# ScalarE's copy of the turned runs between the scalings of two merge tiles, and VectorE's exponentials' low part after the values' low part

## What is computed

```python
x_cat = concatenate([node_feat[src], node_feat[dst], edge_feat], axis=-1)
r = x_cat @ Wr.T + br
q = (node_feat @ Wq.T + bq).reshape(n, H, D)
k = (r @ Wk.T + bk).reshape(e, H, D)
v = (r @ Wv.T + bv).reshape(e, H, D)
a = einsum('ehd,ehd->eh', q[dst], k) * scaler
amax = segment_max(a, dst)
ae = exp(a - amax[dst])
asum = segment_sum(ae, dst)
out = segment_sum(v * (ae / asum[dst])[..., None], dst).reshape(n, H * D)
```

## Time and profile before

| | us |
|---|---|
| median of 3 runs | 1853.32 |
| lowest and highest run | 1849.9, 1858.21 |
| profiled execution, its own time | 1842.91 |
| its span, first to last instruction | 1841.1 |
| busy in it: PE | 1623.5 (88%) |
| DVE | 1296.4 (70%) |
| ACT | 1026.3 (56%) |
| POOL | 697.5 (38%) |

### The profile page before, as it was taken

How to read it: one execution, slowest core, us unless ns; L and a number is a source line. 1 busy time by engine, 2 the same in 40 slices (tenths; PEclk the granted TensorE clock), 3 DMA queues, 4 the chain that set the end, 5 groups by cost and what they waited for, 6 DMA issues and landing times. The chain is left out here.

```text
span 1841.1 us, 26829 instructions
## 1 busy us (share of the span) xinstructions
PE 1623.5 (88%) x7162; PEld 1189.9 (65%) x7162; DVE 1296.4 (70%) x3259; ACT 1026.3 (56%) x3674; POOL 697.5 (38%) x723
## 2 busy tenths in 40 slices
PE   7989979999999999999999999999993777888523
PEld 6867767777777777777777777777772333444311
DVE  5875728887888878887888788878883455322688
ACT  3882225777677777777777767776773344100011
POOL 0001224555555555555555555555551000000033
PEclk9999989999999999999999999999995888999855
DMA  5664327566666666666666666666653324000001
GB/s 181 205 227 154 124 86 238 194 207 212 208 205 201 216 211 207 199 217 212 210 201 212 213 216 199 213 215 201 214 161 130 128 88 137 0 1 0 23 12 44
DMA packets 129670, 300.28 MB, mean 163 GB/s; under 512 B 29088, under 2 KB 50727, under 8 KB 129522
## 3 DMA queue, kind: packets, MB, share of 16 engines
q0 software_dynamic: 63600, 180.17, 29.1%
q1 hardware_dynamic: 60738, 107.59, 19.4%
q10 hardware_dynamic: 5184, 10.81, 1.6%
HBM read 271.40 MB, written 66.58 MB: 184 GB/s over the span
## 5 line engine op out<-in xcount | busy, mean ns | idle before, releaser
L1196 ACT ACTIVATE wv<-vv,expd 128x64 f32<-128x64 f32 x1256 | 316.6, 334 | 2.8
L1208 ACT ACTIVATE old<-old,expd 128x64 f32<-128x64 f32 x1256 | 307.7, 334 | 0.0
L1140 POOL DMA_INDIRECT merge<-new,put_id x157 | 161.1, 1026 | 273.7 <-DVE new L1366 242.1
L1409 PE MATMUL psK<-M_hi,efT_hi 128*128 128x512 f32 x628 | 253.4, 403 | 6.4 <-ACT efT_hi L1166 6.4
L1409 PE MATMUL psV<-M_hi,efT_hi 128*128 128x512 f32 x628 | 255.9, 408 | 0.0
L1410 PE MATMUL psV<-M_lo,efT_hi 128*128 128x512 f32 x628 | 249.7, 398 | 0.0
L1410 PE MATMUL psK<-M_lo,efT_hi 128*128 128x512 f32 x628 | 249.2, 397 | 0.0
L1111 POOL DMA_INDIRECT old<-merge,dst_id x157 | 156.0, 994 | 138.3 <-DMA merge<-new,put_id 112.6
L1111 POOL DMA_INDIRECT kv<-kv_table,src_id x157 | 157.1, 1001 | 72.7 <-issue 47.8
L1182 ACT ACTIVATE expd<-diff 128x32 f32<-128x32 f32 (+1 forms) x79 | 18.1, 229 | 293.9 <-DVE diff L1347 293.9
L1111 POOL DMA_INDIRECT qc<-q_table,dst_id x157 | 155.6, 991 | 53.0 <-issue 46.9
(11 more groups left out here) (271 smaller groups left out, 3404.6 us busy)
## 6 DMA issues: line engine op xcount, KB each, us to landing
efT<-in_ef_turned_dram SPq DMA_DIRECT2D x78, 512.0 KB, 5.0
merge<-empty ACTq DMA_DIRECT2D x4, 2640.0 KB, 9.7
rows<-merge SPq DMA_DIRECT2D x40, 264.0 KB, 3.7
row_block<-dst_rows POOLq DMA_DIRECT2D x13, 768.0 KB, 5.8
dst_line<-dst_rows SPq DMA_DIRECT2D x78, 128.0 KB, 2.7
end_line<-end_rows SPq DMA_DIRECT2D x78, 128.0 KB, 4.1
kv_table<-kv_out SPq DMA_DIRECT2D x10, 512.0 KB, 3.2
raw<-in_L_gnn_Wr_dram SPq DMA_DIRECT2D x12, 256.0 KB, 5.1
```

Source lines behind the costliest of these rows:

```text
L1140: pool.indirect_dma_start(out=merge[2 * (p % 2) + u][:, :], out_offset=bass.IndirectOffsetOnAxis(ap=put_id[:, t:t + 1], axis=0), in_=new[p ...
L1196: act.activation(wv[:, u, h * DH:(h + 1) * DH], vv[p % 2][:, u, h * DH:(h + 1) * DH], ACT.Copy, scale=expd[p % 2][:, u, 0, h:h + 1]).then_ ...
L1208: act.activation(rows, rows, ACT.Copy, scale=expd[p % 2][:, u, 1, h:h + 1]).then_inc(old_scaled, 1)
L1409: pe.matmul(out[:, :], efT_hi[b][:, u, c, :], Me_hi[:, c, col:col + D], start=c == 0, stop=False)
```

## The change

In ACT's loop scale_old takes one tile instead of a pair. The copy of the runs stands between the scaling of the first and of the second old tile; before, it stood behind both. In DVE's loop the low part of the weighted values of pair p - 2's first tile comes ahead of the low part of its exponentials; before, behind it. Instructions, shapes, buffers and waits of each instruction stay as they are.

```diff
-            def scale_old(p):
-                for u in range(tiles_of(p)):
-                    act.wait_ge(old_in[p % 2], landed(p))
-                    for h in range(H):
-                        rows = old[p % 2][:, u, h * DH:(h + 1) * DH]
-                        act.activation(rows, rows, ACT.Copy, scale=expd[p % 2][:, u, 1, h:h + 1]).then_inc(old_scaled, 1)
+            def scale_old(t):
+                p, u = t // 2, t % 2
+                act.wait_ge(old_in[p % 2], landed(p))
+                for h in range(H):
+                    rows = old[p % 2][:, u, h * DH:(h + 1) * DH]
+                    act.activation(rows, rows, ACT.Copy, scale=expd[p % 2][:, u, 1, h:h + 1]).then_inc(old_scaled, 1)
...
                 if p >= 2:
-                    scale_old(p - 2)
+                    scale_old(2 * p - 4)
                 if 1 <= p <= PAIRS:
                     copy_runs(p - 1)
+                if p >= 2 and tiles_of(p - 2) == 2:
+                    scale_old(2 * p - 3)
+                if 1 <= p <= PAIRS:
                     weights(p - 1)
                     weigh_v(2 * p - 2)
                     weights_high(p - 1)
...
                 if older:
+                    wv_low_part(2 * p - 4)
                     exp_low_part(p - 2)
-                    wv_low_part(2 * p - 4)
```

## The result

| | median, us | lowest to highest | runs |
|---|---|---|---|
| before | 1852.97 | 1849.90 to 1858.21 | 4 |
| after | 1944.65 | 1932.88 to 1956.42 | 4 |

The ratio is 1.0492, 95% interval 1.0421 to 1.0562. The forecast was 1819.1 us, range 1808 to 1833. The record does not say on which chip either ran. The lines of after on DVE and PE stand 3 further down than in before (turn_runs L1448, spread_top L1457, the last four matmuls of a product L1416); ACT's and POOL's are unchanged.

What follows compares the result with a forecast made beforehand. A closed chain of ACT and DVE waits was taken to set the 14.22 us period above PE's 13.745 us. Closing it over 72 periods at 0.475 us saves 34.2 us, from the 1853.3 us median to 1819.1 us, range 1808 to 1833.

Steps and rivals of the forecast that it cites:

- PE's floor: PE's own period per pair of tiles, read from early pairs: 13.745 us, against 14.220 us later in the loop.
- the hole in front of spread_top: PE's late delay before spread_top, 1.33 against 0.93 us; with 0.07 us at the next product, 0.47 us a pair to regain.
- the sum: Whole loop: 72 periods x 0.475 us = 34.2 us gained, taken off the median of 1853.3 us.
- ACT's way to PSUM and back: ACT's switch from scaling to copy and back: 0 to 0.26 us a pair, taken at nothing; without cover 20 us.
- The swap on DVE: DVE's wv_lo before exp_lo: gains DVE 0 to 0.2 us, worth nothing on PE; 16 us at most if DVE-bound.
- GpSimd and the queues: GpSimd's merge chain, 8.77 plus 3.7 us landing, fits in 13.745 us; dearer pairs near the end cost 0, at most 2 us.
- Rival C: GpSimd's merge chain: later DMA landings stretch the period to 14.5 us, costing 20 us, 1873 us in all; chance 3%.
- PE becomes the bound: Loop period: DVE's 11.7, the ACT and DVE chain's 12.3 to 12.6, GpSimd's 12.5 us all fall under PE's 13.745.
- the copy of the runs waits more than 1.4 us for PE: On ACT, a sign that the forecast is wrong; a wait of only a few tenths was expected.

Runs made afterwards that it cites:

- e1: After with DVE's old order put back, so only ACT's copy of the runs is moved against before; 1806.19 us, ratio 0.9800 to before, on chip A.
- e2: Before with only DVE's swap (wv_lo ahead of exp_lo); 1843.05 us, ratio 1.0007 to before, on chip A.
- e11: Before with GpSimd's fetches of kv put ahead of those of old; 1923.71 us, ratio 1.0331 to before, on chip E.
- e3b: After with GpSimd's fetch of old held until PE has done the pair's keys, run on chip C; ratio 0.9823 to before.
- e9: After with GpSimd's fetches of q put behind those of old and kv; 1823.22 us, ratio 0.9813 to before, on chip E.
- e4b: After with SyncE's load of the next pair's features issued ahead of the pair's index rows; ratio 1.0076 to before, on chip C.
- e5: After without the features' loads from pair 2 on (tiny loads instead, output wrong); 1883.0 us, ratio 1.0185 to before, on chip D.
- e10: After with GpSimd's wait for the pair's keys put ahead of the fetches of kv; ratio 1.0008 to before, on chip E.
- e3: After with GpSimd's fetch of old held until PE has done the pair's keys, run on chip A; ratio 0.9807 to before.

## Why the prediction was wrong, step by step

**PE's floor, the hole in front of spread_top, the sum: right.** In e1 the 72 periods from 344.77 to 1334.29 us take 13.743 us each; forecast 13.745. The gain was forecast at 34.2 us; chip A gave 1842.3 - 1806.2 = 36.1, and the cured versions on C, D and E 30.7, 32.8 and 29.1 (medians). DVE waits 71.1 / 57 + 28.4 / 56 = 1.75 us a pair for PE, forecast 2.0; ACT 3.3 us for diff, forecast 3.

**ACT's way to PSUM and back: right.** The scaling after the copy starts 798.94 - 798.87 = 0.07 us later, and its eight take 2.01 us, as the eight before the copy do (2.00). The bound of 0.26 us was not needed. The Trainium skill ("Advanced Engine Details and Errata", The Read-Write Bubble) says that on ScalarE and VectorE memory latency shows as a bubble between instructions. The prediction drew from it that the split could cost time; the page does not say that, since the split adds no instruction, and no run here shows a cost.

**The swap on DVE: right** (e2, 1.0007).

**"GpSimd and the queues": this step failed.** It said "No DMA is added or moved" and took 856.49 - 847.72 = 8.77 us for the length of GpSimd's chain. 1.62 us of that are the wait for the put, in a row between those two that the prediction does not show and that stands above (855.24). I asked only whether the chain fits into 13.745 us. I did not ask what becomes of a wait inside it once the engine is freed. It goes like this: before, the puts are issued at 848.70 and 850.02, 5.5 and 4.2 us ahead of turn_runs (854.18), and SyncE's loads at 850.19 to 851.8 come right behind them: the first put leaves 1.5 us ahead of the first load, the second 0.2 us. In e1 they go out at 790.88 and 792.21, 7.4 and 6.1 us ahead of 798.29, while SyncE's first load has moved by 0.5 us only (850.19 to 854.18, now 793.81 to 798.29). Both puts are now at least 1.5 us ahead of the first load, and their landing falls. The lines are those of the puts, 500 to 1300 us, before and in e1:

```profile
DMA to landing us min/median/max: 2.2/4.0/6.8
```

```profile
DMA to landing us min/median/max: 2.2/2.3/5.6
```

In before the median of 4.0 hides two kinds: the first puts of the pairs land in 2.3 us, the second ones in 4.8; in e1 both land in 2.3. In e1 the second put thus lands at about 794.5, before GpSimd has issued the second fetch of q (794.95), the gap closes, and four and four become eight. On a chip where such rows go with late signals of PE, DVE gets the keys late, and runs_lo and spread_top come late behind them. The sum had no term for that; between the two profiled executions it measured 113 us.

**Rival C: right engine, wrong mechanism.** It had the loss come through a later landing, after 1.7 us more, for 20 us and 3%. In e1 the puts' landings got shorter, not longer; the traces of the losing chips give no landing times for the puts. The price was 92 us (medians).

**"PE becomes the bound": true in 38 of 78 periods.** In the others the sign that I had named appeared, "the copy of the runs waits more than 1.4 us for PE": 3.60 us in the pair shown, though it was the wait for the keys beside it that cost the time. I gave it no chance of its own, since nothing in the trace of before hints at it: of PE's 932 signals in its loop none comes over 0.5 us after the recorded end. As that trace is of chip A's kind, it could not have hinted at it. The Trainium skill ("Perfetto Trace Analysis", Tensor Engine Instruction (MATMUL, LD_WEIGHTS)) says that TensorE's recorded end is computed, and that the semaphore update follows only once PSUM has acknowledged the writes. The trace agrees that the two can part, by 4.2 us in the pair shown; the page gives no size.

**The range.** It rested on one execution of before. That the kernel before differs by 0.6% between chips (1842.3 to 1854.3 us) did not announce that the loop with ACT's move would differ by 7% (0.980 for e1 on A, 1.049 for after). One sign was there: the profiled execution was 10.4 us faster than the median of the runs. The prediction carried the 10.4 us along as scatter between runs. It was probably the chip, since before took 6 to 12 us more on B to E than on A.

**What stays open.** Shown: the row makes a loss in before (e11), its removal cures after (e3b, e9), moving or leaving out the features' loads beside it cures part (e4b, e5), and on chip A nothing of it is seen with rows just as long. Not shown: what in the chip holds PE's signals back, why chip A differs, and why rows of six differ between e9 and e10. One rival stands untested: every execution on record has a granted clock and a span of its own, so all seem to have been recorded by the profiler, and exactly on the chips that lose, some 10000 of 26000 semaphore events are missing. Whether the loss would be there without the recording, no run shows. That the row triggers the loss holds for the executions on record either way.

## What to carry to other kernels

When a change frees an engine that issues DMAs, list the waits inside its lap and ask which of them vanish: a gap that looked like waste, here 1.6 us on GpSimd, can be what keeps its issues apart. Read "remote" in the waits as a sign that the record and the semaphores have parted, and look at what GpSimd did in the 10 us before. Count the semaphore events of two traces before you compare them, and be wary of a profiled execution that is faster than all its runs. Run a change that lengthens such a row on more than one chip before you believe its ratio, and prefer an order whose own dependences keep a wait in the row (e9) to one in which it depends on how fast a transfer lands (before).

## What the hardware showed that I had not expected

- PE's signals arrive up to 4.2 us after the recorded ends of their matmuls in the pair shown, several in one heap (801.08 to 801.26 us), while PE goes on with its list. DVE's do not (none of 1339 over 0.5 us late in the same trace), ACT's hardly (7 of 1666).
- This stands behind rows of indirect DMAs from GpSimd, eight of them every 1.25 to 1.3 us: 67 of 71 such rows in e11, 42 of 63 in after, and none of 72 in e1 on chip A.
- In the pair shown PE did nothing for 1.55 us, and soon after its granted clock was 0.50 for 3.4 us; that is 1.6 of the 3.77 us that the pair loses.
- A put's landing depends on how far it leaves ahead of SyncE's loads: 2.3 us in the median when it is 1.5 us or more ahead, 4.8 us when it is 0.2 us ahead (before; in e1 both puts are 1.5 us or more ahead and land in 2.3). The lead is not all: in e3 the puts have the same leads as in e1 and land in 3.2 us.
